# Second feed-forward layer computed transposed, its residual added by VectorE and turned back by transposes

## The reference

```python
x = _layernorm(x + attn_out, ln1_g, ln1_b)
ff = jax.nn.relu(x @ W1.T + b1) @ W2.T + b2
x = _layernorm(x + ff, ln2_g, ln2_b)
```

## Time and profile before

| | us |
|---|---|
| median of 3 runs | 1314.69 |
| the runs | 1313.65, 1314.69, 1317.10 |
| span of the profiled execution, the time it is read with here | 1313.1 |
| PE busy | 1054.3 |
| ACT busy | 806.3 |
| DVE busy | 786.5 |
| POOL busy | 727.8 |

### The profile page before, as it was taken

The page is one execution under the profiler, slowest core; times in us unless marked ns, Lnnn a source line. Parts: engine busy times, 40 slices in busy tenths (PEclk is TensorE's granted clock), DMA queues, the critical chain, the costliest instruction groups (busy, mean ns, idle before and its releaser), DMA issues.

```text
span 1313.1 us, 30142 instructions
## 1 busy us (share of the span) xinstructions
PE 1054.3 (80%) x11425; PEld 454.7 (35%) x11486; DVE 786.5 (60%) x3039; ACT 806.3 (61%) x1032; POOL 727.8 (55%) x743
## 2 busy tenths in 40 slices
PE   0125586169869699999999989998999999989884
PEld 0112341024324243444344334433443334334332
DVE  6866856736766776877686768686245342322323
ACT  1130155057756487778777867787778777866551
POOL 4775755567746567766776677667775750000000
PEclk9997788598989799999999999999999999999997
DMA  6753427335442645364536554643272332000000
GB/s 180 243 132 101 126 74 194 117 92 118 131 127 83 180 106 154 112 179 109 151 116 175 114 150 119 173 109 103 86 145 64 102 111 69 4 17 9 10 8 10
DMA packets 104519, 144.52 MB, mean 110 GB/s; under 512 B 17992, under 2 KB 77136, under 8 KB 104336
## 3 DMA queue, kind: packets, MB, share of 16 engines
q1 hardware_dynamic: 68352, 62.67, 15.6%
q0 software_dynamic: 22816, 44.61, 15.1%
q10 hardware_dynamic: 13168, 34.88, 8.2%
HBM read 124.79 MB, written 12.85 MB: 105 GB/s over the span
## 4 chain that ended last, share of the span: by engine, by line
PE 51%; DVE 20%; ACT 10%; issue 8%; POOL 6%; DMA 3%; DVEq 1%; SPq 0%; ACTq 0%; POOLq 0%
PE sc L1536 15%; PE cb L1556 10%; ACT probs L1317 9%; PE sc L1540 5%; PE m L1613 4%; PE m L1626 4%; DVE agg L912 3%; DVE cand L746 3%; POOL nb_low L638 2%; DVE keys L742 2%; PE m L1438 2%; POOL nb_low L618 2%; DVE st L683 1%; PE sc L1578 1%; PE m L1624 1%
## 5 line engine op out<-in xcount | busy, mean ns | idle before, releaser
L1317 ACT ACTIVATE probs<-sc 128x1024 f32<-128x1024 f32 x512 | 496.4, 1021 | 284.5 <-PE sc L1540 280.0
L618 POOL DMA_INDIRECT nb_low<-h_rows,lsorted x474 | 469.0, 989 | 221.4 <-issue 124.8
L1556 PE MATMUL cb<-probs,va 128*17 128x512 f32 x2048 | 274.1, 608 | 1.8 <-ACT probs L1317 1.1
L912 DVE TENSOR_REDUCE agg<-nb_low 128x128 f32<-128x1024 f32 (+6 forms) x64 | 115.1, 1798 | 102.3 <-DMA nb_low<-h_rows,lsorted 87.3
L1536 PE MATMUL sc<-q_near,k_g 32*128 32x512 f32 x1024 | 149.8, 655 | 25.1 <-ACT probs L1317 21.9
L1536 PE MATMUL sc<-q_far,k_g 32*128 32x512 f32 x1024 | 148.8, 650 | 23.2 <-ACT probs L1317 21.5
L1540 PE MATMUL sc<-barred,negident 32*32 32x512 bf16 x4096 | 112.8, 391 | 0.0
L746 DVE MAX8 cand<-keys 128x8 f16<-128x128 f16 x512 | 105.4, 279 | 2.2
L638 POOL DMA_INDIRECT nb_low<-h_rows,first_lists x80 | 80.0, 1000 | 44.0 <-issue 23.5
L1540 PEld LDWEIGHTS sc<-barred,negident 32*32 32x32 bf16 x4096 | 35.3, 88 | 199.0 <-issue 199.0
L1333 ACT ACTIVATE m<-adj_m 128x1024 bf16<-128x1024 int32 x64 | 67.8, 1059 | 46.7 <-DMA adj_m<-in_adj_dram 46.4
(11 more groups left out here) (186 smaller groups left out, 1506.6 us busy)
## 6 DMA issues: line engine op xcount, KB each, us to landing
adj_t<-in_adj_dram SPq DMA_DIRECT2D x64, 512.0 KB
adj_m<-in_adj_dram ACTq DMA_DIRECT2D x64, 512.0 KB
nb_low<-h_rows,lsorted POOLq DMA_INDIRECT x474
xh<-in_x_dram SPq DMA_DIRECT2D x8, 512.0 KB, 6.5
h_rows<-xh SPq DMA_DIRECT2D x8, 512.0 KB
hl<-h_rows SPq DMA_DIRECT2D x8, 512.0 KB
x<-in_x_dram SPq DMA_DIRECT2D x16, 256.0 KB
out_dram<-h2T SPq DMA_DIRECT2D x16, 256.0 KB
```

The lines of the kernel that those rows point to most:

```text
L618: pool.indirect_dma_start(out=dst, out_offset=None, in_=h_rows[0:(f + 1) * (N + 1), :], in_offset=bass.IndirectOffsetOnAxis(ap=lsorted[:, ...
L912: ch.link(nc.vector.tensor_reduce(a, first.rearrange("p k c -> p c k"), AX.X, ALU.max))
L1317: nc.scalar.activation(probs[:, i % 2, 2 * pair:2 * pair + 2, :], sc[:, 2 * pair:2 * pair + 2, :], ACT.Exp, scale=SCALE).then_inc(s_probs, 1)
L1556: last = nc.tensor.matmul(cb[a * SPAN:a * SPAN + VW, :], va[:, u % 2, a, kt, :], probs[:, i % 2, a, :], start=(kt == 0), stop=(kt == T - 1))
```

## The change

`forward` puts W2 on the stationary side and streams 512 nodes of `hid` at once: 4 matmuls in place of 21 per half, with the result transposed (channels on partitions). ACT's copy of the turned norm now applies ln1_g and ln1_b as per-partition scale and bias, so that `turned` holds the true residual; the bias row, the diagonal, and the folding of ln1 at the start are gone. DVE's new `add_input` adds b2 and the residual to the result and writes the sum over `turned`; PE's new `turn_sum` turns it back by four transposes into the same bank, and `finish` goes on from there.

```diff
+SUM_AT, EARLY_SUM_AT = [{14}, {18}], {31}
+def layer_done(p, h):
+    return 4 * p + 2 * h + 1
+def sum_turned(p, h):
+    return 4 * p + 2 * h + 2
+def layer_taken(p, h):
+    return (2 * p + h) * (TH + 1) + 1
+def sum_taken(p, h):
+    return (2 * p + h + 1) * (TH + 1)
...
# DVE, setup
-                    ch.link(nc.vector.tensor_tensor(stage_rows[:, B12, :], stage_rows[:, B12, :], stage_b2, ALU.add))
...
-                    ch.link(nc.vector.tensor_scalar(diag1[:, :], identf[:, :], g1c[:, 0:1], None, ALU.mult))
-                    nc.vector.tensor_tensor(b1c[:, :], b1c[:, :], m[:, 0, 0:FC], ALU.add).then_inc(s_setup_dve, 1)
...
# DVE
+                def add_input(p, h):
+                    dve.wait_ge(s_ffn_ready, layer_done(p, h))
+                    half = turned[:, h * HALF:(h + 1) * HALF]
+                    nc.vector.scalar_tensor_tensor(out=half, in0=m[:, h, :], scalar=b2c[:, 0:1], in1=half, op0=ALU.add, op1=ALU.add).then_inc(s_ffn_used, 1)
...
-                    dve.wait_ge(s_ffn_ready, 2 * p + h + 1)
+                    dve.wait_ge(s_ffn_ready, sum_turned(p, h))
...
                         merge_pair(2)
+                    if live(p) and s < B:
+                        add_input(p, 0)
                     if live(f):
                         pool_tile(f, 7)
                     if live(p) and s < B:
                         finish(p, 0)
...
                     if live(p):
+                        add_input(p, 1)
                         finish(p, 1)
...
                     if s == B - 1:
+                        add_input(g, 0)
                         finish(g, 0)
...
# ACT
+                def norm_out(p, h):
+                    act.wait_ge(s_nT_ready, 2 * p + h + 1)
+                    nc.scalar.activation(turned[:, h * HALF:(h + 1) * HALF], m[:, h, :], ACT.Identity, bias=ln1_col[:, 1:2], scale=ln1_col[:, 0:1]).then_inc(s_nT_sb, 1)
...
# PE
                     if part == 0:
                         refill(half)
-                        bias_rows(half, B12)
-                    pe.wait_ge(s_hid_sb, 2 * FC * p + (half + 1) * FC)
-                    for t in range(2 * part, 2 * part + 2):
-                        o = m[:, half, t * C:(t + 1) * C]
-                        cols = slice((half * TH + t) * P, (half * TH + t + 1) * P)
-                        nc.tensor.matmul(o, turned[:, cols], diag1[:, :], start=False, stop=False)
-                        for k in range(FC):
-                            last = nc.tensor.matmul(o, hid[:, k, t * P:(t + 1) * P], w2T[:, k, :], start=False, stop=(t == TH - 1 and k == FC - 1))
+                    for k in range(2 * part, 2 * part + 2):
+                        pe.wait_ge(s_hid_sb, 2 * FC * p + half * FC + k + 1)
+                        last = nc.tensor.matmul(m[:, half, :], w2T[:, k, :], hid[:, k, :], start=(k == 0), stop=(k == FC - 1))
                     if part:
                         last.then_inc(s_ffn_ready, 1)
-                    freed[half] = (s_ffn_used, T * p + (half + 1) * TH)
+                    freed[half] = (s_ffn_used, layer_taken(p, half))
+
+                def turn_sum(p, h):
+                    refill(h)
+                    for t in range(TH):
+                        last = nc.tensor.transpose(m[:, h, t * C:(t + 1) * C], turned[:, (h * TH + t) * P:(h * TH + t + 1) * P], identf[:, :])
+                    last.then_inc(s_ffn_ready, 1)
+                    freed[h] = (s_ffn_used, sum_taken(p, h))
...
                             forward(e, h, at[n])
+                        for e, h, _ in closing(s, n, SUM_AT, EARLY_SUM_AT):
+                            turn_sum(e, h)
```

More of the change, by code:

```diff
@@ L47 @@
 SORT_BANK = (2, 1)
-L0B, BO, B12 = range(3)
+L0B, BO = range(2)
 G2, B2R = range(2)
@@ L159, in program @@
         w2T = sb("w2T", [P, FC, C])
-        diag1 = sb("diag1", [P, C])
-        bias_t = sb("bias_tiles", [P, 3, C], bf16)
+        bias_t = sb("bias_tiles", [P, 2, C], bf16)
         rows = sb("bias_rows", [P, 2, C])
@@ L166, in program @@
         b1c = sb("b1c", [P, FC])
-        g1c = sb("g1c", [P, 2])
+        ln1_col = sb("ln1_columns", [P, 2])
+        b2c = sb("b2c", [P, 1])
         xh = sb("xh", [P, T, C])
@@ L240, in program @@
         list_rows = lst[:, :, :].bitcast(fp16)[:, :, 0:COUNT + 1]
-        stage_part = wstage[:, 3200:3584].bitcast(bf16).rearrange("p (k j c) -> p k j c", k=2, j=3)
+        stage_part = wstage[:, 3200:3456].bitcast(bf16).rearrange("p (k j c) -> p k j c", k=2, j=2)
         sc = ctx.enter_context(nc.psum_tensor("sc", [P, 4, HALF], fp32))
@@ L334, in program @@
         VA_LOADS = 16 * (2 * GROUP - 1)
-        W_LOADS = 16 * (1 + 3 + 1 + FC + 1 + 2 + 4 + 2 * 2 * GROUP + FC + 2 + 1)
+        W_LOADS = 16 * (1 + 3 + 1 + FC + 1 + 2 + 2 + 2 * 2 * GROUP + FC + 3 + 1)
         def live(g):
@@ L726, in bias_tiles @@
                     ch.link(nc.vector.tensor_copy(bqk_abs[:, :, 0], pmax[:, :]))
-                    dve.wait_ge(s_weights_ready, 5)
+                    dve.wait_ge(s_weights_ready, 4)
                     ch.link(nc.vector.tensor_tensor(stage_rows[:, BO, :], stage_rows[:, BO, :], m[:, 1, 0:C], ALU.add))
@@ L1268, in load_vectors @@
                         act.dma_start(rows[:, j, :], v.rearrange("(a n) -> a n", a=1).to_broadcast([P, C])).then_inc(s_w_in, 16)
-                    for j, v in ((L0B, L0_b), (BO, bo), (B12, ln1_b)):
+                    for j, v in ((L0B, L0_b), (BO, bo)):
                         act.dma_start(stage_rows[:, j, :], v.rearrange("(a n) -> a n", a=1).to_broadcast([P, C])).then_inc(s_w_in, 16)
-                    act.dma_start(stage_b2, b2.rearrange("(a n) -> a n", a=1).to_broadcast([P, C])).then_inc(s_w_in, 16)
                     act.wait_ge(s_setup, 3)
@@ L1281, in load_vectors @@
                     for j, v in ((0, ln1_g), (1, ln1_b)):
-                        act.dma_start(g1c[:, j:j + 1], v.rearrange("(p a) -> p a", a=1)).then_inc(s_w_in, 16)
+                        act.dma_start(ln1_col[:, j:j + 1], v.rearrange("(p a) -> p a", a=1)).then_inc(s_w_in, 16)
+                    act.dma_start(b2c[:, :], b2.rearrange("(p a) -> p a", a=1)).then_inc(s_w_in, 16)
                     act.dma_start(bvc[:, :], bqkv[2 * C:3 * C].rearrange("(p a) -> p a", a=1)).then_inc(s_w_in, 16)
@@ L1293, in setup @@
                     act.wait_ge(s_weights_ready, 2)
-                    nc.scalar.activation(stage_w1, sc[:, 1, :], ACT.Copy)
-                    nc.scalar.activation(w1T[:, :], sc[:, 1, :], ACT.Copy, scale=g1c[:, 0:1]).then_inc(s_wT_sb, 1)
+                    nc.scalar.activation(w1T[:, :], sc[:, 1, :], ACT.Copy).then_inc(s_wT_sb, 1)
                     act.wait_ge(s_weights_ready, 3)
@@ L1346, in hidden @@
                     if half and k == 0:
-                        act.wait_ge(s_ffn_ready, 2 * p + 1)
+                        act.wait_ge(s_ffn_ready, layer_done(p, 0))
                     nc.scalar.activation(hid[:, k, :], m[:, bank, :], ACT.Relu, bias=b1c[:, k:k + 1]).then_inc(s_hid_sb, 1)
@@ L1386, in _ @@
                         for e, h, _ in closing(s, n, NT_AT, EARLY_NT_AT):
-                            half_out(turned[:, h * HALF:(h + 1) * HALF], h, s_nT_ready, 2 * e + h + 1, s_nT_sb)
+                            norm_out(e, h)
                         for e, h, at in closing(s, n, HID_AT, EARLY_HID_AT):
@@ L1449, in setup @@
                     pe.wait_ge(s_wT_sb, 3)
[L1450 to L1453, removed]
                 def value_bias():
```

9 lines of the change are left out of this document (3 added, 6 removed).

## The result

The changed kernel needs 1335.56 us in the median of five runs (1322.63 to 1339.19) where the kernel before needed 1314.69 (also in the median of five, with two runs more than in the table above): a ratio of 1.0151, 95% interval 1.0115 to 1.0186. The runs scatter over 16.6 us, those of before over 3.5 (in later sets of 17 to 21 runs over 7.1 to 8.5), and the profiled execution is the fastest of the five: span 1320.5 us, only 7.4 more than before.

What follows compares the result with a forecast made beforehand. PE's side work was taken as the bound from slot 2 on. Slots 1 to 4 add 18.0 and 10.6, slots 5 and 6 -0.8, slot 7 -0.5, tail +4.0, prologue -0.7: 1314.7 + 30.6 = 1345 us, range 1329 to 1357.

Steps and rivals of the forecast that it cites:

- The wide products: PE's two `forward` steps per half: each lasts 4.33 us like a `hidden` pair, saving about 1.15 us per half.
- The wait in step 14, slot 1: PE before `turn_sum(p, 0)`: step 15 starts 17.3 us later, the old 11.22 us wait in step 17 goes; net 4.0 us.
- the 6.65 of the sum: Slot 1's forecast lengthening: 4.0 us net wait plus 2.65 us for slow clock, PE's saving, transposes and step 20.
- The wait in slots 2 to 4: PE idle in step 14 before `turn_sum(p, 0)`, behind DVE's list merge and addition: 5.7, 4.9 and 3.8 us.
- where they started at: Step 15's scores in slots 2 to 4: at 568.8, 698.1 and 827.8 us, where they started at 563.30, 693.36 and 824.14.
- the wait is paid once: Rival: DVE comes earlier in slots 2 to 4, so only slot 1, step 20 and the tail cost; 1322 us, chance 0.1.
- The clock: PE behind the waits of slots 1 to 4 runs at the lower clock, adding 2.4 us in each slot.
- The rival of the clock that stays up after waits under 6 us: Rival: no slow clock after those waits, 3 times 2.9 us and the tail's 1.4 less; 1335 us, chance 0.12.
- Step 20: PE wants bank 2 before DVE finishes `finish(p, 1)` and `context(g, 1)`: new wait of 0.9 us in slots 1 to 6.
- The tail: After slot 7, `context(7, 3)` stands behind the later `finish(7, 0)`: +2.9, slow PE +1.4, very end -0.3; +4.0 us.
- The prologue: Before slot 1, three small DVE operations fewer and others narrower: -0.7 us (0 to -1.3).

Runs made afterwards that it cites:

- `again`: The changed kernel run once more, unedited: 1333.42 us, ratio 1.0142 to the kernel before.
- `early_sum`: Changed kernel with the second `turn_sum` in step 17 instead of 18 and the early one in step 30 instead of 31: 1326.29 us, ratio 1.009.
- `early_add`: Changed kernel with DVE's `add_input(p, 0)` moved behind `merge_pair(0)`, ahead of later list work, in slots 1 to 4: 1315.83 us, ratio 1.0011.
- `late_add`: Changed kernel with DVE's `add_input(p, 0)` moved later, behind `pool_tile(f, 7)`: 1349.1 us, ratio 1.0264 to the kernel before.
- `short_beta`: Changed kernel with POOL's addition of the second norm's bias cut to 8 columns of one tile: 1325.74 us, ratio 1.0087 to the kernel before.
- `both`: Changed kernel with `add_input(p, 0)` behind `merge_pair(0)` in slots 1 to 4 and `turn_sum` in steps 14, 17 and early 30: 1313.94 us, ratio 1.0001.

## Why the prediction was right, and where it was not

- *The wide products.* Forecast 4.33 us per forward step. Measured 4.33 (547.28 to 551.61 to 555.94). Steps 11, 12, 15 and 16 of slot 5 are shorter by 0.64, 0.51, 0.64 and 0.51 us: a half saves 1.15 us, as said.
- *The wait in step 14, slot 1.* Forecast about 17 us of idle time, with step 15 starting 17.3 us later; measured 17.32 us idle, and step 15 starts 17.0 us later, both counted from step 9. The 11.22 us wait in step 17 is gone, and slot 1 is 6.85 us longer for the 6.65 of the sum.
- *The wait in slots 2 to 4.* Forecast 5.7, 4.9 and 3.8 us. The first profile shows 0.81, 1.95 and 1.16, `again` 0.79 in slot 2 and 5.30 and 3.60 in slots 3 and 4. The step that failed is "where they started at" DVE's time of before: I took the merge's times for fixed and they held a 3 us delay that comes and goes. The list work ended at 562.23 us in slot 2 of the first profile, where I had 567.02: 3 us is the hold, and 1.9 us the gather of `agg`, which began at 541.29 us (541.34 in `again`) and not at 543.19, though slot 2 began at the same time. In place of 22 us these three slots cost 4.5 in the first profile and 14.4 in `again` (0.9 + 8.4 + 5.1).
- *The rival "the wait is paid once"* (1322 us, chance 0.1) had exactly this condition, that DVE comes earlier in slots 2 to 4, and the first profile's 1322.63 us is that case. I had the wrong reason for it (POOL and DMA catching up) and dismissed it by the gather alone. The median lies nearer to the forecast than to the rival, because DVE is held again in most runs that were profiled; that was not in the forecast's reasoning, and so far the hit is luck.
- *The clock.* Half speed behind the 17.32 us wait, for 5 us, as forecast; behind the waits of 0.81 to 1.95 us full speed. With real waits of 5 us it falls too (below). The rival of the clock that stays up after waits under 6 us is refuted: the clock fell behind every wait of `turn_sum` of 3.4 us and more, and twice behind waits of about 2 us (below). That the median, 1335.56 us, is just what this rival gave (1335) is chance.
- *Step 20.* Forecast 0.9 us, measured 1.30 to 1.54 in slots 1 to 6. Slots 5 and 6 nevertheless are shorter by 0.8 and 0.4 (forecast 0.4 each): step 20 of slot 5 lasts 1.4 us longer, but steps 17 and 19, which the sum left out, are 0.4 and 0.2 shorter.
- *The tail.* Forecast +4.0; from step 26 of slot 7 on +4.9, with a wait of 4.71 us. `early_sum` gave back 4.7 by the placing of one sum: the cause is as said, `context(7, 3)` behind `finish(7, 0)`.
- *The prologue.* Forecast -0.7; measured -6.8. I had counted the operations that left DVE and forgotten that two loads left ACT's queue which were issued ahead of SP's third load of `adj_t`; they are worth 4 us at DVE's first maximum. How the 6.8 us come about stays open: the prologues of the profiles without these loads reach from 386.9 to 391.7 us, those of the unedited kernel before are 393.8 and 395.2.

In sum: the forecast is 9.4 us above the median. Against `again`, whose profiled run lies near the median, the sum is 13.3 us too high (30.6 against 17.3), and two of its terms make that up: the prologue (6.2) and slot 2 (7.2), where DVE was not held and came 1.9 us sooner besides. The mechanism that decides, PE put behind DVE's lists, is shown by `early_add`, which moves one operation of 0.75 us on DVE and takes 17.6 us off, and by `late_add`, which moves it the other way and adds 15.7.

## What to carry to other kernels

Before an engine is made to wait for an operation, ask what stands ahead of that operation in its queue, and how much of that time scatters from run to run: here the change lost most of its 20 us not by the work it added but by the place of one 0.75 us addition, and with the places of the addition and of the transposes behind it chosen by slot it gained 0.5%. Slack that a schedule has can also hide its scatter: the kernel before spread over 7 to 8.5 us in sets of 17 to 21 runs, the changed one over 16 in five or six. And when a few operations leave, count the transfers that leave with them.

## What the runs showed of the hardware

- *A DVE operation held by a POOL operation.* A 0.17 us operation of DVE lasts 2.5 to 3.1 us when POOL's addition of 128x1024 floats (2.35 to 2.39 us) starts 0.06 to 0.7 us after it, and ends 0.04 us after the addition. TENSOR_SCALAR, TENSOR_TENSOR and SCALAR_TENSOR_TENSOR on 8 columns were held; MAX8, which reads one tensor, was not. The Trainium skill ("SBUF — State Buffer", Who interferes with whom) says that DVE and GpSimd share one pair of ports as an exclusive lock, that a DVE instruction with one SBUF input outside the two-port modes doesn't contend, and that the blocked one waits for the whole instruction. The trace agrees for the operations with two inputs and for MAX8. The held TENSOR_SCALAR has one input too; the same section counts it among those that can enter a two-port mode, but no view shows the mode. In four profiles a longer DVE operation with two inputs (SCALAR_TENSOR_TENSOR, 1.2 us) had been under way for 0.8 to 1.0 us when POOL's addition came; it kept its length, and the addition lasted 2.50 to 2.65 us. I hadn't weighed all this in the forecast. Which of the operations was caught changed from run to run, which is where the changed kernel's scatter comes from at least in part; that it is all of it was not shown (`short_beta` still spreads over 11 us).
- *The granted clock behind a wait of PE.* Behind waits up to 3.60 us the four transposes of `turn_sum` took 0.65 to 0.67 us, behind 4.08 us and more 1.11 or 1.12 (4.08, 4.33, 4.90, 5.28, 5.30, 5.42, 6.26, 7.12, 9.2, 15.0, 17.3, 19.7). That doesn't mean that the shorter waits were free: within the next 4.3 us the clock fell behind the waits of 3.43, 3.57 and 3.60 us (0.60 to 0.65 over that stretch), behind one of 2.18 in slot 3 of `short_beta` (0.60) and one of 1.91 in slot 5 of `late_add` (0.67), and it stayed up behind one of 2.98 in `both` and one of 1.95 in the changed kernel (1.00). So the length of the wait alone doesn't tell. In slot 3 of `short_beta` the step behind the transposes lasted 5.90 us, in the changed kernel 4.33. Windows of `again` (length, busy of PE, PEld, DVE, ACT, POOL, PEclk, DMA share, GB/s), behind the waits of 5.30 and 3.60 us, of the changed kernel behind 17.32 and 1.95, and of `short_beta` behind 2.18 and `both` behind 2.98:

```profile
698.64:702.90 4.26, 4.26 (x32) 1.53 (x36) 3.54 (x17) 0.50 (x1) 1.98 (x2) 0.50 0.04 15
836.13:840.50 4.37, 4.37 (x36) 1.03 (x36) 3.37 (x16) 1.60 (x2) 1.94 (x2) 0.64 0.05 17
```

```profile
429.50:434.50 5.00, 4.92 (x36) 1.54 (x36) 4.17 (x21) 1.16 (x2) 2.51 (x3) 0.50 0.07 20
695.80:700.00 4.20, 4.20 (x39) 1.67 (x40) 3.49 (x16) 2.07 (x3) 2.75 (x3) 1.00 0.22 65
```

```profile
696.43:700.70 4.27, 4.27 (x36) 1.23 (x36) 3.55 (x17) 0.97 (x2) 1.98 (x2) 0.60 0.04 15
```

```profile
843.95:848.30 4.35, 4.35 (x51) 2.16 (x52) 3.21 (x21) 2.31 (x4) 3.44 (x4) 1.00 0.75 208
```

0.50 is the lower level, 1.2 GHz. So the step from a wait of 2 us to one of 5 cost 6.6 us in slot 3 (132.6 to 139.2), twice what the wait grew by.
- *Two loads of 64 KB*, issued by ACT, delayed the third load of `adj_t` by 4 us (20.59 to 24.71), though their data isn't used. ACT issued them at 12.73 and 13.21 us, SP the load at 14.55; from 16 to 20 us the DMA engines moved 80 to 139 GB/s with the two loads and 258 to 409 without, busy for 0.85 of the time or more in both.
